# Four-layer cross-attention kernel: the last group's layer 3 cut into two halves of four sequences, and layer 3's stages at other places in the groups before it

## What is computed

```python
xa = _ln(x, ln1_w, ln1_b)                    # needs the whole output of layer 2
xxx = jnp.tanh((xa + sx * maa_x) @ maa_w1)   # then five mixes, and w, r, k, v, g from them
def step(s, rkvw):
    r_t, k_t, v_t, w_t = rkvw
    a = k_t[..., :, None] * v_t[..., None, :]
    out = jnp.einsum('bhi,bhij->bhj', r_t, u * a + s)
    s = a + w_t[..., :, None] * s
    return (s, out)
_, out = jax.lax.scan(step, s0, rkvw)        # over the 64 positions
x1 = x + og * g @ Wo.T                       # og: out, normalized in each head
xc = _ln(x1, ln2_w, ln2_b)
return x1 + rr * (kk @ Wfv.T)                # rr, kk: a gated two-matrix block on xc
```

## Time and profile before

| | us |
|---|---|
| median of 3 runs | 1861.78 (1856.99 to 1864.47) |
| the profiled execution | 1861.21, its span 1859.5 |
| first block (group 0, no layer 3) | 189.0 |
| seven blocks with layer 3 of the group ahead | 218.1 to 221.7 each |
| last block, layer 3 alone | 136.7 |
| PE, DVE, ACT, POOL busy | 88%, 65%, 50%, 41% of the span |

### The profile page before, as it was taken

The page is one execution under the profiler, slowest core; times in us unless marked ns, Lnnn a source line. Parts: engine busy times, 40 slices in busy tenths (PEclk is TensorE's granted clock), DMA queues, the critical chain, the costliest instruction groups (busy, mean ns, idle before and its releaser), DMA issues.

```text
span 1859.5 us, 34983 instructions
## 1 busy us (share of the span) xinstructions
PE 1631.7 (88%) x13711; PEld 1040.7 (56%) x13711; DVE 1217.2 (65%) x2153; ACT 932.5 (50%) x1881; POOL 766.6 (41%) x871
## 2 busy tenths in 40 slices
PE   5888898899998898898988989988998989889735
PEld 3566555565565655665556645656556555556303
DVE  3743579655885568845687557865588466982483
ACT  4444554555555645556455555455455564555202
POOL 5631248404573147702486034840457214770000
PEclk8999999999999999899999989999999989999857
DMA  6001024200421005110142103410042100510070
GB/s 188 2 2 37 1 26 53 44 19 1 51 39 35 19 1 70 25 29 19 22 49 35 33 6 36 53 36 19 1 58 36 31 19 1 70 25 1 13 92 12
DMA packets 73569, 60.81 MB, mean 33 GB/s; under 512 B 38960, under 2 KB 56512, under 8 KB 73408
## 3 DMA queue, kind: packets, MB, share of 16 engines
q1 hardware_dynamic: 55648, 47.99, 18.2%
q10 hardware_dynamic: 17216, 10.55, 2.0%
q0 software_dynamic: 544, 0.03, 0.0%
HBM read 20.28 MB, written 4.19 MB: 13 GB/s over the span
## 4 chain that ended last, share of the span: by engine, by line
PE 66%; DVE 13%; ACT 9%; POOL 6%; issue 4%; ACTq 1%; DMA 0%; DVEq 0%; SPq 0%; POOLq 0%
PE bank L638 24%; PE bank L777 8%; PE bank L1040 6%; DVE late L1339 5%; PE bank L977 5%; PE bank L654 3%; PE bank L1002 3%; PE bank L910 2%; PE bank L717 2%; POOL soft_ring L1708 2%; PE bank L801 2%; ACT soft_ring L1170 2%; PE bank L792 2%; PE bank L995 2%; POOL late L1663 2%
## 5 line engine op out<-in xcount | busy, mean ns | idle before, releaser
L1708 POOL TENSOR_TENSOR soft_ring<-soft_ring,seg_max 128x512 f32<-128x512 f32 x256 | 278.7, 1104 | 262.9 <-DVE seg_max L1505 261.9
L1185 ACT ACTIVATE soft_ring<-soft_ring 128x512 f32<-128x512 f32 x256 | 160.1, 625 | 177.9 <-POOL soft_ring L1708 177.9
L1339 DVE TENSOR_TENSOR_SCAN late<-late 128x520 f32<-128x520 f32 x128 | 213.6, 1669 | 9.9 <-POOL late L1665 6.1
L1663 POOL TENSOR_TENSOR late<-late 128x520 f32<-128x520 f32 x112 | 171.2, 1529 | 76.3 <-DMA late<-late 41.3
L777 PE MATMUL bank<-early 32*128 32x128 f32 (+2 forms) x1024 | 154.4, 420 | 43.4 <-ACT soft_ring L1170 40.7
L977 PE MATMUL bank<-ident,soft_ring 128*128 128x128 f32 x1024 | 164.7, 290 | 17.2 <-ACT soft_ring L1185 13.8
L977 PEld LDWEIGHTS bank<-ident,soft_ring 128*128 128x128 f32 x1024 | 118.0, 146 | 90.3 <-issue 55.7
L1505 DVE TENSOR_REDUCE seg_max<-soft_ring 128x8 f32<-128x512 f32 (+1 forms) x256 | 166.0, 674 | 0.2
L1674 POOL COPY late<-edge 128x8 f32<-128x8 f32 x16 | 3.2, 199 | 330.3 <-DVE late L1443 330.2
L1068 ACT ACTIVATE late<-bank 128x512 f32<-128x512 f32 (+2 forms) x104 | 61.3, 595 | 154.9 <-PE bank L638 154.6
L1716 POOL TENSOR_SCALAR soft_ring<-soft_ring,rden 128x256 f32<-128x256 f32 x64 | 59.5, 929 | 173.0 <-DVE rden L1467 173.0
(11 more groups left out here) (263 smaller groups left out, 3420.6 us busy)
## 6 DMA issues: line engine op xcount, KB each, us to landing
late<-late SPq DMA_DIRECT2D x128, 260.0 KB, 4.4
c<-in_ctx ACTq DMA_DIRECT2D x8, 512.0 KB, 3.9
x<-in_x ACTq DMA_DIRECT2D x8, 512.0 KB, 4.9
out_x<-late SPq DMA_DIRECT2D x8, 512.0 KB, 2.9
mask<-in_mask_Bx1xSxS_ff ACTq DMA_DIRECT2D x16, 128.0 KB, 3.9
mask<-in_mask_BxS_ik SPq DMA_DIRECT2D x8, 256.0 KB, 3.6
w<-in_L_xattn_mlp_w SPq DMA_DIRECT2D x2, 1024.0 KB, 9.1
wkv<-in_L_xattn_kv_w SPq DMA_DIRECT2D x1, 512.0 KB, 4.2
```

The lines of the kernel that those rows point to most:

```text
L1185: af(soft[:, u % SOFT, :], soft[:, u % SOFT, :], ACT.Exp).then_inc(sig("exp"), 1)
L1339: nc.vector.tensor_tensor_scan(sj[:, n % 2, :], wP[:, k, :, :].rearrange("p b t -> p (b t)"), aj[:, n % 2, :], 0.0, ALU.mult, ALU.add).the ...
L1663: tt(aj[:, n % 2, :], kP[:, k, :, :].rearrange("p b t -> p (b t)"), vj[:, n % 3, :], ALU.mult).then_inc(sig("kv_done"), 1)
L1708: tt(s, s, seg_max[:, u % SOFT, 0:segs].unsqueeze(2).broadcast_to([128, segs, 512 // segs]), ALU.subtract).then_inc(sig("sub"), 1)
```

## The change

It has two parts.

The last block's layer 3 is worked as two halves of four sequences. A class `Part` holds the views of one half: tiles, statistics, semaphores of its own (those of the second half begin with `b_`). The first half lies in `late`, the second in `early`. All instructions on such a tile have half the columns (256 in place of 512, a scan of 260 in place of 520). The value buffers `vj` are six for each half in place of three. The two halves use six banks in turn ("alone") and two for the sums of lanes ("held"). A list `alone` merges the 48 stages of both halves into one order, with the second half 10 time units behind the first, and all engines take it, SP too: it issues a half's first six spreads at its "bonus", and each later one at a scan stage. The store is made in two pieces.

In the other blocks the tiles and instructions stay the same, and `PLACES` and `SCAN_PLACES` hold other numbers.

```diff
-        RINGS = {"score": [0, 1], "turn": [2, 3, 4, 5], "late": [6, 7]}
+        RINGS = {"score": [0, 1], "turn": [2, 3, 4, 5], "late": [6, 7], "alone": [2, 3, 4, 5, 0, 1], "held": [6, 7]}
...
+        whole = Part("", "", late, 0, NB, 5168, 3, "late", "late")
+        parts = (Part("first half", "", late, 0, NB // 2, 6144, 6, "alone", "held"),
+                 Part("second half", "b_", early, NB // 2, NB // 2, 6144, 6, "alone", "held"))
...
-            "variance": (128, 128, 125, 122),
-            "gate": (130, 129, 125, 123),
-            "project": (131, 133, 125, 128),
...
+            "variance": (127, 128, 122, 121),
+            "gate": (132, 130, 124, 121),
+            "project": (132, 133, 126, 127),
...
+        PRE, SCAN = STAGES.index("bonus") + 1, STAGES.index("center")
+        TIMES = ([1.4 * n for n in range(PRE)] + [1.4 * PRE + 1.4 * n for n in range(SCANS)] +
+                 [1.4 * (PRE + SCANS) + 2.0 * n for n in range(len(STAGES) - SCAN)])
+        BEHIND = 10.0
+        alone = [(P, stage) for _, _, P, stage in sorted(
+            [(at + BEHIND * n, n, P, stage) for n, P in enumerate(parts) for at, stage in zip(TIMES, STAGES)], key=lambda s: s[0:2])]
...
                 def rest():
+                    if now is None:
+                        for P, stage in alone:
+                            layer3(stage, P)
+                        return
                     while count[0] <= LAST:
                         step()
...
+                    else:
+                        for P, stage in alone:
+                            if stage == "bonus":
+                                for n in range(P.depth):
+                                    spread_values(n, P)
+                            elif stage[0] == "scan" and P.depth <= stage[1] + P.depth < KT * HS:
+                                spread_values(stage[1] + P.depth, P)
+                            elif stage == "ffn v":
+                                store(P)
```

More of the change, by code:

```diff
@@ new lines, in sync_program @@
+                    if now is not None:
+                        for n in range(KT * HS):
+                            spread_values(n, whole)
+                        store(whole)
+                    else:
[7 more added lines that the diff above has]
+                                store(P)
@@ L743, in tensor_program @@
+                        project("Wfv", P.kkT)
                 step, rest = beside(layer3, "PE")
```

512 lines of the change are left out of this document (273 added, 239 removed), and 8 rows, old and new, of the table SCAN_PLACES.

## The result

The changed kernel takes 1817.5 us (median of 4 runs, 1816.5 to 1820.1), the kernel before beside it 1863.1 us (median of 4 runs, 1857.0 to 1865.3). The ratio is 0.976, with a 95% interval of 0.974 to 0.979: 46 us less. The prediction was 1827, 34 us less than its reference of 1861.2.

What follows compares the result with a forecast made beforehand. It took PE's work plus some 18 us idle to bound seven blocks, a PE-ACT-DVE chain the last, with DVE full during scans. 1861.2 - 17 (last block) - 17.5 (places) = 1827 us, range 1806 to 1850.

Steps and rivals of the forecast that it cites:

- Part 1: Last block worked in two halves: 119 us worked out, 120 taken in place of 136.7, so -17 us.
- g: Last block, first half: this stage, ahead of "r u k", the first spread and "bonus", done at 30 us.
- first scan: Last block, first half: the recurrence's first scan at about 34 us, before at about 55; 20 us won.
- Part 2: New table of places in the seven other blocks, only order changes: -2.5 us per block taken, -17.5 for seven.
- discount: Seven blocks: -3.9 us each worked out, taken as -2.5 because freed time partly comes back at the next wait.
- `xnT` with the product: PE's wait for DVE's normalization, one scan stage ahead of the masks: -2.7 us per block, POOL's product wait included.
- MEMSET and pick: POOL's MEMSET leaves the stretch ahead of a subtraction, a pick fills PE's wait for `hT`: -0.7 us per block.
- The projection: PE's projection one matmul pair later covers its wait for the gate: -0.5 us per block.
- The table gives nothing: Rival: in the seven blocks every wait is replaced by a neighbouring one, only the last block gains: 1844 us, chance 0.24.
- Spreads: Rival: half-size DMA packets cost the same and set the last block's pace, 131 us: 1838 us, chance 0.07.
- Halves that do not overlap: Rival: last block stays at 137 us; 1844 us with Part 2, 1861 without; chance 0.06 for both.
- The thirteenth product: Rival: on POOL it waits for DVE's scan, delaying subtractions and PE 4 us per block: 1872 us, chance 0.05.

Runs made afterwards that it cites:

- e5: Changed kernel with the second half 20 time units behind the first in the order list, not 10: 1833.9 us, ratio 0.986.
- e3: Changed kernel with DVE's scan (with reading and emptying) and POOL's thirteenth product put back to their old places in the seven blocks: 1839.6 us, ratio 0.987.
- e11: Changed kernel with only POOL's MEMSET of layer 2's values put back behind five more products: 1817.4 us, ratio 0.977.
- e12: Changed kernel with the rear stages' places (from center to the last ffn product) as before: 1820.8 us, ratio 0.979.
- e2: Kernel before with the two new tables of places, last block in one piece: 1835.1 us, ratio 0.985.
- e7: Changed kernel with the whole second half behind the first, no stages mixed: 1862.8 us, ratio 1.002.
- e8: Changed kernel with DVE's scan put back behind the last masks, POOL's thirteenth product left early: 1851.8 us, ratio 0.995.
- e6: Changed kernel with no lag between the halves in the order list (0, not 10): 1826.0 us, ratio 0.982.
- e4: Changed kernel with five stages moved in the last block's order so that ACT loads its table four times fewer: 1814.9 us, ratio 0.975.
- e9: Changed kernel with second half's early stages moved forward and, behind the scans, the first half's stages put later: 1816.3 us, ratio 0.976.

## Why the prediction came out as it did

**Part 1, by its own steps.** "g" drained at 31.3 (worked out: 30), first scan 36.6 (34), the second half's first scan 53.5 (49), the first half's last reading ends at 75.7 (74), the second half's at 87.2 (86), then 31.8 us (33), the block 118.9 (119, taken 120). DVE's work 85.5 us (86), a half step 1.33 (1.36). The loads in the block are seven, and one ends 3.5 us ahead of it: the eight of the forecast.

Three steps are off by more than 2 us. The first mix comes at 10.4 and not at 8: table load, two `maa` products and tanh took 5.2 us where I had 2.4, the first product alone 3.9 at a clock of 0.50. The stretch from there to "g" was 1 us shorter than worked out. From "g" to the first scan it took 5.2 us and not 4, and in all that scan is 2.6 late. The second half's scans start 4.5 late: DVE spends longer on the second half's mixes and the first half's steps in turn than I had put; that cost nothing, since DVE was full either way. So the sum of 119 owes something to errors that cancel.

That the halves overlap was right, but my reason was only half of it. I counted on the early first scan; e5 has it as early and takes 14 us more, so an early scan is not enough. The lags differ in how long DVE stands idle at the two ends (32.6, 43.3 and 43.0 us with a lag of 10, 20 and 0).

**Part 2.** The working was right in its sum and its main term, and the discount was wrong. I worked out -3.9 per block and took -2.5, because "what is freed at one wait partly comes back at the next". The blocks gave -3.86. Part did come back, but at `xnT` my 2.7 held the new wait at the turn already. The picks, which I named in the discount, do wait longer (12.1 us in place of 3.8), and in e3, where the other waits are back, they have 8.8; other waits went in exchange, the one for `hT` fell from 7.3 to 3.3 us and the one for the divide, 4.4 before, is gone. By term:
- `xnT` with the product: worked out 2.7, measured 2.8 at the start of `xnT`; with what follows up to the centering 3.3 (e3, "to center") or 2.9 (e3, by time). The picture that I gave, 1 to 2 us left at `xnT` and 1 new at the turn, is what the trace shows (1.6 to 2.2 and 0.8).
- MEMSET and pick: worked out 0.7, not shown (e11); with both back at the other place the stretch is already as long as before.
- The projection: worked out 0.5, measured 0.6 (e12).

That the three add up to the measured 3.9 is in part luck: 0.7 for MEMSET and pick that is not there stands against 0.5 behind `xnT` that I did not have and 0.1 more at each of the other two.

**The rivals.** The table gives nothing: refuted by e2. Spreads: refuted, below (by its own 0.234 us a packet a spread of 128 takes 1.9 us of 16 engines and not 2.0). Halves that do not overlap: e7 builds them in the extreme, and it would have cost more than I had said, 28 us above the block in one piece. The thirteenth product: it did wait as I wrote, for a scan that DVE starts only after two maxima, 1.2 us where I had 0.8. What failed was its price. The subtractions behind it are late, but PE, which had idled there anyway, loses 0.8 us at the turn and not 4. With the scan behind the masks the mechanism does reach PE (e8).

**What stays open.** Why the blocks of one kernel differ by up to 3.8 us in one execution (213.6 to 217.4), with the same order: PE's busy time in these two is 196.7 us at a clock of 0.98 and 201.0 at 0.96, but why the clock differs is not shown. And whether PE's 2.05 us at 773.78, which the trace puts to no releaser, is the same wait as the 1.64 us at `xnT` in other blocks; that it is missing where the other stands speaks for it.

## What to carry over

When a phase with one full engine lies between two phases of short hand-overs, cut it in independent halves and choose the offset so that the full engine's other work fits the gaps at both ends; measure the offset, since 10 units to either side cost 9 and 14 of 46 us here. When an instruction is moved on one engine, look for the one on another engine that it waits for: without the scan's move the product's cost 2 us a block, with it it gained up to 1.6, and the scan's move alone gained 1.3. And do not take a discount for "it comes back elsewhere" when the later wait already stands in the sum.

## What the runs showed of the hardware

- **Packets of half the size took half the time.** From 1735 to 1775 us (queue, packets, MB, share of 16 engines; answers to the earlier trace rows):

```profile
q1 hardware_dynamic: 3744, 3.45, 61.7%
```

  61.7% of 16 x 40 us over 3744 packets is 0.105 us for a mean of 921 bytes, against 0.234 us for 1849 bytes before (the engines were busy 84.3% of the time then, so the load differs as well). Between its scans DVE nowhere waited for a spread (the longest gap for ACT is 0.26 us); ahead of each half's first product it stood 0.4 and 0.5 us with no releaser shown, 3.4 us after the first spread was issued. The Trainium skill (page "DMA: Bandwidth & Descriptors", section "Why small descriptors are slow (HBM only)") says that transfers from SBUF to SBUF don't have the penalty of small descriptors; at these two sizes the traces agree.
- **One group of matmuls has two durations.** Eight 128x256 records behind a wait, and eight later in the same block:

```profile
1701.29 3.92 PE L690 MATMUL bank<-late,maa 128*128 128x256 f32 x8 [2.06 <-DVE late L1443]
...
1724.70 1.99 PE L690 MATMUL bank<-late,t_Wg 128*128 128x256 f32 x8
```

  The granted clock is 0.50 in the first and 1.00 in the second, the 1.2 and the 2.4 GHz level; in the scans of e6 and e7 it is 0.50 throughout. The projection of the first half stood at the high level in the changed kernel and near the low one in e4, which costs 1.6 us. Such groups may be a part of e4's and e9's misses of 3 to 5 us; how large a part is not shown.
- **The mean clock did not tell the time.** Two runs of the changed kernel took 1816.9 us at a mean granted clock of 0.959 and 1818.1 at 0.947; the mean block is 215.4 us in the changed kernel (0.959) and in e4 (0.950).
